# Four attention layers over 32 images: another table of step times sets the order on every engine

## The reference, cut to what matters

```
# L0 (L2 is the same with an instance norm, and no output projection)
attn = softmax(einsum('bnd,bmd->bnm', q, k) * C ** -0.5)
out  = einsum('bnm,bmd->bnd', attn, v) @ Wp.T + bp;  x = out + xn
# L1, eight heads
attn = softmax(einsum('bhqd,bhkd->bhqk', q, k));  o = einsum('bhqk,bhkd->bhqd', attn, v)
x = o @ wp.T + bp + x
# L3
tailor = 1 / (N + Qn . (Kn.sum(-1) + EPS));  out = gamma * (V.sum(-1) + Qn . (Kn V)) * tailor
```

## Time and profile before

| | |
|---|---|
| median of 3 runs | 6187.2 us (6186.26 to 6193.69) |
| the profiled execution's own time | 6179.77 us |
| its span | 6178.0 us |
| PE busy | 5741.7 us, 93% of the span |
| DVE, ACT, POOL busy | 4620.2, 4141.6, 3426.0 us |

### The profile page before, as it was taken

How to read it: one execution, slowest core, us unless ns; L and a number is a source line. 1 busy time by engine, 2 the same in 40 slices (tenths; PEclk the granted TensorE clock), 3 DMA queues, 4 the chain that set the end, 5 groups by cost and what they waited for, 6 DMA issues and landing times.

```text
span 6178.0 us, 82441 instructions
## 1 busy us (share of the span) xinstructions
PE 5741.7 (93%) x28818; PEld 2690.0 (44%) x28818; DVE 4620.2 (75%) x5748; ACT 4141.6 (67%) x5764; POOL 3426.0 (55%) x2739
## 2 busy tenths in 40 slices
PE   5789999999999999999999999999999999999885
PEld 2334444444444444444444444444444444444332
DVE  2677777777777777777777777777777777777752
ACT  2367777766777676777766767767677777677652
POOL 4336655556665555655555666555565555566433
PEclk7899999999999999999999999999999999999996
DMA  1011101011101101111101110110110110111000
GB/s 36 4 27 24 29 21 30 20 31 24 31 19 30 31 20 31 24 25 25 29 21 31 24 31 19 30 30 21 31 24 21 29 30 20 31 24 31 16 17 8
DMA packets 103485, 154.27 MB, mean 25 GB/s; under 512 B 63776, under 2 KB 66080, under 8 KB 102944
## 3 DMA queue, kind: packets, MB, share of 16 engines
q1 hardware_dynamic: 103072, 149.00, 11.1%
HBM read 18.13 MB, written 16.78 MB: 6 GB/s over the span
## 4 chain that ended last, share of the span: by engine, by line
PE 72%; DVE 16%; ACT 5%; issue 3%; POOL 3%; DMA 0%; SPq 0%; DVEq 0%; POOLq 0%; ACTq 0%
PE p_max L1251 16%; PE p_chain L1251 15%; PE p_sc L1251 12%; PE p_full L1251 11%; PE p_acc L1251 9%; PE p_head L1251 8%; DVE mx_half L1066 8%; ACT p L930 3%; DVE f2mx L1061 2%; DVE fp L1107 2%; POOL x L787 1%; POOL fsum L781 1%; POOL fp_lo L760 1%; DVE f_num L1125 1%; DVE t_dn L1198 1%
## 5 line engine op out<-in xcount | busy, mean ns | idle before, releaser
L1066 DVE TENSOR_REDUCE mx_half<-p_max 128x2 f32<-128x1024 f32 x2048 | 2506.8, 1224 | 891.1 <-PE p_max L1251 883.1
L930 ACT ACTIVATE p<-p_head 128x1024 f32<-128x1024 f32 x2048 | 2094.8, 1023 | 1103.0 <-PE p_head L1251 1047.8
L760 POOL TENSOR_TENSOR fp_lo<-fp,fp_hi 128x512 fp32r<-128x512 f32 x1024 | 1311.6, 1282 | 734.1 <-ACT fp L894 732.5
L781 POOL TENSOR_TENSOR fsum<-fsum,fp 128x512 f32<-128x512 f32 x768 | 987.9, 1286 | 282.3 <-ACT fp L894 282.1
L1251 PE MATMUL p_max<-ks,qs 63*128 63x512 f32 x4096 | 993.9, 481 | 102.0 <-DVE mx_half L1066 80.3
L1251 PE MATMUL p_acc<-p,v 128*17 128x512 f32 x8192 | 1080.9, 601 | 7.8 <-ACT p L930 7.6
L1251 PE MATMUL p_head<-qs,ks 64*128 64x512 f32 x4096 | 938.9, 454 | 43.6 <-ACT p L930 26.5
L892 ACT ACTIVATE fp_hi<-fp 128x512 fp32r<-128x512 f32 x1024 | 641.4, 626 | 367.3 <-DVE fp L1107 261.6
L1107 DVE TENSOR_TENSOR fp<-p_sc,f_shifts 128x512 f32<-128x512 f32 x1024 | 700.1, 684 | 147.5 <-PE p_sc L1251 60.3
L1251 PEld LDWEIGHTS p_max<-ks,qs 63*128 63x128 f32 x4096 | 385.8, 185 | 921.5 <-DVE mx_half L1066 736.3
L1251 PEld LDWEIGHTS p_head<-qs,ks 64*128 64x128 f32 x4096 | 385.7, 185 | 679.5 <-issue 385.8
(11 more groups left out here) (187 smaller groups left out, 7977.6 us busy)
## 6 DMA issues: line engine op xcount, KB each, us to landing
qs<-cq_hi SPq DMA_DIRECT2D x128, 256.0 KB, 4.8
ks<-ck_hi SPq DMA_DIRECT2D x128, 256.0 KB, 4.7
x_in<-x_dram SPq DMA_DIRECT2D x32, 512.0 KB, 4.4
qs<-cq_lo SPq DMA_DIRECT2D x64, 256.0 KB, 4.4
ks<-ck_lo SPq DMA_DIRECT2D x64, 256.0 KB, 5.1
out_dram<-x SPq DMA_DIRECT2D x32, 512.0 KB, 5.3
o<-o SPq DMA_DIRECT2D x256, 32.0 KB, 2.0
zrow<-rz SPq DMA_DIRECT2D x128, 16.0 KB
```

The source lines that it names most:

```text
L760: pool.tensor_tensor(fp_lo[u % 2][:, :], fp[u % 2][:, :], f32(fp_hi[u % 2][:, :]), ALU.subtract).then_inc(f.plo, 1)
L781: pool.tensor_tensor(dst, dst, fp[u % 2][:, :], ALU.add).then_inc(f.sum, 1)
L930: act.activation(p1[slot][:, 2 * pr:2 * pr + 2, :], P_HEAD[:, :].rearrange("p (e n) -> p e n", e=2), ACT.Exp, scale=float(DH) ** -0.5).the ...
L1066: dve.reduce_max(mx_half[:, pr, :, t, kh], P_MAX[:, :].rearrange("p (e n) -> p e n", e=2), AX.X)\
```

## The change

Only numbers change: `PERIOD`, `FIRST`, `FINAL`, and all 661 entries of `TIME`. `STEPS`, the steps' code, buffers and semaphores are the same, and so are all instructions and DMAs. The new numbers are whole multiples of 0.311, each used by one step of a period. In the middle of the run 285 PE steps stand in one period. 228 of them stand in the same order as before; most of the others pass one to three neighbours.

```
-PERIOD = 206.000
+PERIOD = 205.571
...
-    m_turn=[-3.213, 116.801],
+    m_turn=[443.378, 554.716],
...
-FIRST = [-0.019, -0.019, -0.003]
-FINAL = [0.012, 0.017, 0.028]
+FIRST = [0.000, 0.000, 0.000]
+FINAL = [0.000, 0.000, 0.000]
```

More of the change, by code:

```diff
@@ L77 @@
[L77 to L84, removed]
@@ L158 @@
[L158 to L167, removed]
-    t_tokens=[372.077, 374.541, 377.951],
-    t_norms=[379.422],
-    t_keys=[380.954],
-    t_matrix=[390.878],
-    t_keep=[376.906],
-    t_ksum=[395.741],
-    t_scale=[390.327],
-    t_turn=[396.761, 400.053],
@@ L176 @@
[L176 to L179 removed]
+    load=[0.825],
+    g_stat=[91.637],
+    g_average=[109.053],
+    g_var=[101.278],
+    g_apply=[105.632],
+    f_qk=[117.139, 671.652, 121.804, 673.829, 127.091, 676.628, 135.799, 678.494],
+    f_hi=[106.565, 672.896, 109.986, 677.561, 114.34, 678.805, 117.45, 683.47],
+    f_lo=[114.029, 676.006, 114.962, 679.427, 124.914, 680.982, 127.713, 683.159],
+    f_value=[137.976, 684.403, 139.531, 685.336],
@@ new lines @@
+    f_based=[164.722, 688.446, 204.53, 738.206],
+    f_scores=[175.607, 699.642, 178.095, 703.063, 183.071, 715.814, 186.803, 726.388, 190.535,
+        729.187, 193.023, 734.785, 206.707, 742.56, 211.061, 744.737, 215.415, 755, 221.013,
+        758.732, 229.41, 762.464, 234.386, 767.44, 237.496, 769.617, 238.429, 777.392, 239.673,
+        781.746, 246.515, 782.99],
+    f_less=[170.942, 698.087, 177.473, 701.819, 181.827, 717.058, 189.291, 719.546, 196.444,
+        724.211, 198.31, 724.833, 199.554, 736.34, 203.597, 737.584, 212.305, 743.182, 224.434,
+        747.536, 228.788, 755.622, 230.965, 759.354, 232.831, 764.952, 236.252, 766.507, 245.893,
+        772.727, 250.558, 779.569],
@@ new lines @@
+    f_add=[128.957, 720.168, 171.253, 702.13, 172.808, 718.302, 192.712, 721.412, 194.889, 730.12,
+        196.755, 735.718, 202.042, 745.048, 203.286, 748.469, 194.578, 673.207, 209.195, 749.713,
+        214.793, 761.531, 225.056, 763.397, 226.3, 768.684, 237.185, 773.349, 240.295, 776.459,
+        243.094, 783.923],
+    f_pv=[183.382, 711.46, 187.425, 713.015, 190.846, 732.608, 195.822, 736.962, 206.085, 742.871,
+        211.994, 751.268, 212.927, 755.933, 221.635, 757.799, 229.099, 763.708, 233.142, 768.062,
+        238.118, 769.928, 239.051, 776.148, 241.539, 782.679, 245.271, 786.1, 259.266, 786.411,
+        265.797, 791.387],
@@ new lines @@
+    f_move=[216.037, 741.316, 278.237, 783.301],
+    f_sums=[253.046, 796.052],
+    f_row=[255.223, 776.77],
+    f_gather=[153.526, 674.14],
+    f_recip=[258.644, 795.43],
+    f_return=[183.693, 674.762],
+    f_spread=[276.371, 801.961, 279.792, 805.071],
+    f_divide=[270.151, 802.583, 271.706, 806.626],
+    p_stat=[274.505],
+    p_average=[287.567],
+    p_var=[279.17],
+    p_apply=[285.701],
+    p_qk=[293.787, 298.141, 302.495, 304.05],
+    p_hi=[289.122, 293.165, 295.653, 297.83],
@@ new lines @@
+    p_lo=[290.055, 298.452, 303.117, 308.715],
+    p_value=[307.471, 311.514],
+    p_keep=[300.629, 301.562],
+    stack=[252.735, 320.222],
+    m_max=[364.073, 366.561, 369.982, 371.226, 373.092, 374.025, 375.58, 377.135, 380.556, 381.8,
[6 rows of a table added]
+    m_max_read=[355.054, 360.652, 360.963, 361.896, 364.384, 369.049, 369.36, 369.671, 372.47,
[6 rows of a table added]
+    m_both=[437.78, 534.812],
+    m_turn=[443.378, 554.716],
+    m_neg=[439.335, 541.343],
+    m_row=[356.609, 439.024],
+    s_scores=[446.488, 450.22, 451.153, 454.263, 456.44, 457.684, 461.105, 463.904, 466.703,
[6 rows of a table added]
@@ new lines @@
+    s_exp=[448.976, 449.909, 453.019, 453.952, 459.861, 460.172, 461.727, 462.66, 468.88, 472.301,
[6 rows of a table added]
+    s_pv=[455.507, 456.751, 461.416, 467.014, 476.344, 484.43, 487.851, 491.583, 495.937, 502.468,
+        508.377, 522.994, 526.415, 535.434, 548.185, 560.314, 566.845, 573.687, 579.285, 581.773,
+        587.06, 591.725, 592.658, 596.079, 599.811, 621.581, 621.892, 626.868, 633.71, 638.375,
+        646.461, 646.772],
+    s_out=[489.406, 544.764, 603.232, 651.748],
+    o_gather=[465.77, 555.338],
@@ new lines @@
+    o_recip=[585.194, 645.217],
+    o_return=[473.545, 563.424],
+    o_move=[498.425, 556.271],
+    o_spread=[652.37, 656.102],
+    o_divide=[654.858, 658.279],
+    o_project=[657.968, 660.767],
+    o_residual=[660.145, 664.81],
+    i_stat=[666.054],
+    i_apply=[667.92],
+    f_out=[794.497],
+    t_project=[810.047, 815.956, 824.353],
+    t_tokens=[814.09, 815.334, 816.578],
+    t_norms=[819.377],
+    t_keys=[830.573],
+    t_matrix=[834.616],
+    t_keep=[824.975],
+    t_ksum=[837.415],
@@ L181 @@
+    t_scale=[833.994],
+    t_turn=[842.391, 844.257],
+    t_turned=[835.238, 838.037],
+    t_out=[847.367, 853.587],
+    t_leave=[840.836, 858.563],
+    store=[837.104])
 CHAIN_READER = dict(g_average="g_var", p_average="p_var", f_qk="f_hi", p_qk="p_hi",
```

86 lines of the change are left out of this document (16 added, 70 removed), and 48 rows, old and new, of tables (m_max, m_max_read, s_exp, s_scores).

## The result

The changed kernel takes 6290.4 us (median of 6283.54, 6290.44 and 6317.51) against 6187.2: a ratio of 1.0179, with a 95% interval of 1.0165 to 1.0192. It is 1.8% slower, far outside the range of 6156 to 6214. The profiled execution has a span 103.8 us longer than that of before (6281.8 against 6178.0).

A forecast was written before the change was run, and what follows sets the result against it. The prediction took PE's work, its array-shape changes and many short waits to set the 182.85 us period. Terms summed to -0.05 us per period, -1.5 over 31 periods, +1 at the start: about 6186 us, range 6156 to 6214.

The forecast's parts named there:

- First place: `m_max` after the second `t_project`: its 0.48 wait for DVE goes, as the maximum now precedes `f_less`; -0.5 us per period.
- Second place: `f_scores` waiting 0.54 for an `f_less` behind `m_neg`: `m_turn` now comes at once, 0.1 of wait left; -0.4 us per period.
- Third place: Around `g_average`: 0.3 wait for `p_keep(1)`, plus 0.2 and 0.2 from exponentials ahead of `p_keep` and `p_hi`; +0.7 us per period.
- L3's chain: `t_turn`'s 0.68 wait goes, new waits from `t_matrix` on add 1.1; +0.4 us per period, bounds -0.7 to +1.0.
- Where L1 changes image: Around `m_turn` and the 32nd `m_max`: 0.65 of waits go, small waits there and around `o_spread` come; -0.1 us per period.
- PE can't gain from its clock: In the windows of the kernel before, the granted clock is 1.00, already the upper level of 2.4 GHz.
- The slower rival: `s_exp` ahead of the readers of `p_chain` delays it by its whole length; +1.6 us per period, 6237 us, chance 0.25.
- Two `s_scores` with one `s_pv`: Close pairs on PE can't follow in under 1.63 us; four such places instead of three; +0.3 us per period.
- Shapes and other small waits: PE's array-shape changes, -0.1, and small waits at `s_scores`, `m_max` and L2's last `f_scores`, -0.35 us per period.
- the new waits are covered: Faster rival: removed waits stay away; with half the losses the period falls by 0.9 us, giving 6159 us; chance 0.32.

The follow-up runs named there:

- experiment 2: The changed kernel with PE's order where L1's heads change image (27th `m_max` to second `o_project`) as before; 6147.1 us, ratio 0.9933.
- experiment 11: The kernel before, order untouched, with two unused maxima over 128x1024 added on DVE ahead of the 14th `f_less` of L0; 6257.6 us, ratio 1.0114.
- 12: The changed kernel with PE's order from the 27th `m_max` to the second `t_out` as before, and the changed order from `m_turn` on; 6174.2 us, ratio 0.9977.
- 5: The changed kernel with PE's order where L1's heads change image as before, and the stretch around `g_average` as before on ACT and PE; 6162.9 us, ratio 0.9958.
- 10: The kernel before, order untouched, with one unused maximum over 128x1024 added on DVE ahead of the 14th `f_less` of L0; 6206.6 us, ratio 1.0031.

## Why the prediction was wrong

The forecast was no change, from a sum of -0.05 us per period. Two steps failed. Of the rest, the first and second place held, the third came out in its size alone, and L3's chain had the wrong sign.

- **The term "Where L1 changes image" (-0.1) was +2.3.** For this I set the same PE steps of both traces beside each other (periods without a fall), and took the difference between points ahead of which the same steps stand. Counted from the 13th `f_scores`, the 15th starts 1.37 later, the step behind it 1.72 and the next such point, at `o_spread`, 2.31. Against experiment 2, whose table is the same elsewhere, the whole place costs 183.15 - 181.62 = 1.53, for its half ahead of the 13th `f_scores` is 0.5 shorter. I had followed the `stack` to the 32nd `m_max`, where nothing is lost on PE, and `m_turn` and `s_pv`. I did not follow the other chain through this place, `s_pv(3, 7)`, sums, `o_recip`, row, `o_spread`, though the same order moved the `stack` closer to its first transfer, and its last step, `o_spread`, ahead of an `f_pv` of 0.90. On DVE a late `o_recip` also holds up the `f_less` behind it. And I took DVE's instructions at fixed durations, where the trace of before already had them at 0.18 and 0.84.
- **The clock.** "PE can't gain from its clock" was true, and I stopped there: it could lose. That was 86 of the 104 us, and no rival had it.
- **First place** (-0.5): -0.55. **Second place** (-0.4): -0.66, the last 0.1 of wait went too. **Third place** (+0.7): +0.54 in the changed kernel, in part by luck. `g_average` waits the 0.30 that was worked out, but the 0.4 for the exponentials did not come, for `p_value` never waits; what came is the 0.51 of `m_max(52)` for DVE held by POOL, which I did not have. The slower rival, at +1.6, did not come.
- **L3's chain** (+0.4): -0.4. `t_turn`'s wait went (-0.65), and of the 1.1 us of new waits that I walked out only 0.25 came, around `t_matrix`. `ka` was there when PE came to `t_matrix`, and the two maxima ahead of `t_scale` cost nothing. The bound of -0.7 was nearer than the value taken.
- **Two `s_scores` with one `s_pv`** (+0.3): about 0.1. **Shapes and other small waits** (-0.45 together): -0.9, as the difference of the whole, +0.40, and the terms above; 0.3 of it lies in the place where L1 changes image, just ahead of the 13th `f_scores`.

The rival "the new waits are covered" was right about L3's chain, and not about the third place; with the place where L1 changes image as before, the changed table is 0.7% faster.

## What to carry to other kernels

When an order changes, walk every chain that crosses the place, from its first moved step to its last, through DMA queues and the in-order queues that others stand in; the chain that is not walked is the one that bites. Where PE is nearly full, new waits may cost more through the clock than they last: a fall cost 3.9 us here, behind waits of 1.34 and 0.67. Their length doesn't tell whether they will, so read the granted clock of each stretch, and not only the sum of the waits. And read the spread of an instruction's duration, not its mean: the short DVE instructions that sometimes took four to six times as long were held by POOL here, each ending within 0.05 of an instruction of POOL.

## What the runs showed of the hardware that was not expected

- PE's clock fell from 1.00 to 0.50 behind short idle times of PE: some 1.34 and 0.67 us of it in 22 of 29 periods, 1.45 in 7 (experiment 11), 0.66 in 7 (12), 1.21 (5) and 0.33 (10) in none. It then stayed at 0.50 for 10.24 us in most, although PE was busy for 9.86 of them.
- An instruction of DVE over 128x32 took 1.27 us instead of 0.20, ending 0.05 behind an instruction of POOL; with one operand in PSUM it took 0.19 beside the same instruction. One over 128x1 took 1.04 instead of 0.22.
- Matmuls that compute nothing, placed where PE waits, made the changed kernel 79 us faster.
